# Causal mask of the two self attentions by extra contraction rows and small diagonal products, their maximum subtracted without GpSimd

## Chip, cores, metric

The kernel runs on one core of one Trainium2 chip. The metric is the device time of one execution in microseconds (us); lower is better. Most executions of one kernel agree within 0.3%, but the three timed runs of this one differ by more.

## What is computed

The reference is a decoder of two blocks over x of 8 sequences x 128 tokens x 256 features: block 0 is a causal self attention, a long convolution with gates and a mixture of experts; block 1 is a causal self attention, a masked cross attention and a routed mixture of experts. Each sublayer adds to x, behind a layer norm. The part that matters here, for both self attentions (16 heads of 16 features):

```python
scores = jnp.einsum('bqhd,bkhd->bhqk', Q, K)          # 1/sqrt(16) in all
scores = jnp.where(tril(ones(128, 128)), scores, -inf)
attn = softmax(scores, axis=-1)
out = jnp.einsum('bhqk,bkhd->bqhd', attn, V).reshape(B, S, D) @ Wo.T + bo
```

## The kernel before

Five engines run programs of their own, tied by semaphores (`S("name")`). The whole of x stays in SBUF. Order in time: self attention of block 0 (the list `FIRST`, call name SELF0), convolution, experts of block 0, then one pipeline (`SECOND`) that holds self attention of block 1 (SELF1, units from step 0) and cross attention (CROSS, units from step `CROSS_FROM` = 20), then the experts of block 1.

An attention is cut into units. A self attention has two units for each sequence, 16 in all, of eight heads each; the cross attention has 32 units. `attention(run)` of every engine walks the same steps t, and each engine does at step t what its lag says. On TensorE (all matmuls are issued by the helper `mm`, L1396, and f32 transposes by `tr`, L1400), step t does, in this order:

1. `less_max` of unit t-2 (L1521): eight products of 128 columns write minus the row maximum (and the mask) into the banks that take the scores by key. Stationary operand: `LMs`, which GpSimd made; moving: minus the identity, `negidb`.
2. `mask` of unit t (L1490): two products of 512 columns, identity times the mask repeated four times, start banks 0 and 1. Each waits until VectorE has read that bank (`att_mx`).
3. `scores` of unit t (L1511): eight products with 48 contraction rows (three terms of a split float16 product, 16 rows each), four at rows 0 to 47 into bank 0 and four at rows 64 to 111 into bank 1, alternating.
4. `scores_by_key` of unit t-2 (L1533): the same eight transposed, keys on partitions, on top of step 1's banks (2 to 4).
5. Transposes of x for the next sublayer, where due; `pv` of unit t-4 (exponentials times values, four column groups of 32); transposes of its result (lag 5); every second step the transposes and the product of the output projection (lags 6 and 7).

VectorE (`attention`, L1100) divides results, adds to x, takes the maximum over keys from banks 0 and 1 (two reductions, L1141) and does statistics and normalisation of x. ScalarE takes the exponential of banks 2 to 4 (L831) and copies from PSUM. GpSimd (L592) makes `LMs` = maximum minus mask for every unit of every attention (L614, two instructions), then `rstd` (L562, L563), low parts of float16 pairs (L585) and the bias rows (L581). SyncE issues the DMAs: `stack` (L447) waits for each quarter of the queries and keys and spreads it into the rows of `QS` and `KS`, 24 DMAs for each self attention, each into 16 partitions, twelve for each half of the tokens (`spread`, L445); half 0 gates unit 0 and half 1 gates unit 8. The constants (`ident`, `identb`, `negidb`, `causal`, `identh`, then `chgroup` and others) are made at the start on GpSimd (L574 to L645), each adding to `S("const")`.

## Time and profile before

| what | value |
|---|---|
| three timed runs | 585.8, 577.96, 586.9 us; median 585.8 us |
| profiled execution, device time | 583.44 us |
| its span, first to last instruction | 581.7 us (1.7 us lie around it) |
| mean granted TensorE clock | 0.974 |

The profile is one execution. Durations in it are its own; a number worked out from it is set against 583.44 us, not against the median.

### The profile page before, as it was taken

The page shows a single profiled execution, that of the slowest core. Times are in us where ns is not written, and L with a number is a line of the kernel's source. Part 1 is how long each engine was busy: PE and PEld are TensorE (multiplying, and loading weights), DVE is VectorE, ACT ScalarE, POOL GpSimd, SP SyncE. Part 2 cuts the span into 40 slices and gives each one's busy share as a digit, 9 for nine tenths or more (in the row PEclk, how much of TensorE's full clock was granted, in tenths as well). Part 3 has the DMA queues.
Part 4 walks back from the last instruction along what each step waited for, and adds up shares of the span by engine and source line. Part 5 has one row for each costly group of instructions (what it writes and reads, how often), then busy time and mean ns, then how long its engine had stood idle before and what let it go on. Part 6 is the DMA issues. An engine that isn't in the chain of part 4 may idle for free.

```text
span 581.7 us, 12908 instructions
## 1 busy us (share of the span) xinstructions
PE 537.3 (92%) x4838; PEld 338.2 (58%) x4838; DVE 363.7 (63%) x798; ACT 259.8 (45%) x533; POOL 316.2 (54%) x392
## 2 busy tenths in 40 slices
PE   7989998999699999999998889997999998989998
PEld 4546765444436666664665456664555554456687
DVE  5455864999846556452476478768577766963331
ACT  2315463000476666562445435655656567204430
POOL 3437854889664436321021579959899984450000
PEclk9988998999879999998999979999999999999999
DMA  7996019000006434331211995011130003017311
GB/s 251 133 145 257 3 55 406 2 0 0 1 2 187 120 98 108 93 109 68 75 50 25 124 150 220 3 29 29 29 101 1 3 7 158 1 53 306 139 40 64
DMA packets 25133, 53.04 MB, mean 91 GB/s; under 512 B 3515, under 2 KB 16333, under 8 KB 23153
## 3 DMA queue, kind: packets, MB, share of 16 engines
q1 hardware_dynamic: 24357, 51.01, 32.2%
q10 hardware_dynamic: 716, 1.21, 0.6%
q8 instruction: 40, 0.66, 0.5%
q14 instruction: 20, 0.16, 0.1%
HBM read 41.51 MB, written 1.12 MB: 73 GB/s over the span
## 4 chain that ended last, share of the span: by engine, by line
PE 61%; DVE 17%; POOL 8%; issue 4%; SPq 3%; DMA 3%; ACT 3%; POOLq 0%; DVEq 0%; ACTq 0%
PE PS L1396 55%; POOL R L614 6%; PE PS L1400 4%; DVE R L1242 4%; DVE R L1239 3%; SPq L445 2%; DVE mx L1141 2%; DVE R L424 2%; DMA R<-R 1%; DVE xn L1020 1%; DMA WT<-in_wt_a_dram 1%; PE PS L1419 1%; POOL rstd L563 1%; DVE X L1010 1%; DVE stats L1005 1%
## 5 line engine op out<-in xcount | busy, mean ns | idle before, releaser
L1396 PE MATMUL PS<-R 128*128 128x256 f16 (+5 forms) x1864 | 187.2, 277 | 2.2 <-DVE R L1298 1.4
L1396 PEld LDWEIGHTS PS<-R 128*128 128x128 f16 (+4 forms) x1864 | 125.3, 104 | 72.9 <-issue 46.9
L1141 DVE TENSOR_REDUCE mx<-PS 128x4 bf16<-128x512 f32 x128 | 82.3, 685 | 36.6 <-PE PS L1396 27.6
L831 ACT ACTIVATE R<-PS 128x512 f32<-128x512 f32 x128 | 69.4, 594 | 70.6 <-PE PS L1396 70.5
L1396 PE MATMUL PS<-xnT,R 128*128 128x512 f16 (+1 forms) x348 | 87.1, 392 | 2.1 <-ACT xnT L745 2.1
L614 POOL TENSOR_TENSOR R<-mx,causal 128x512 bf16<-128x512 bf16 x64 | 66.9, 1066 | 37.6 <-DVE mx L1141 36.8
L1289 DVE TENSOR_TENSOR R<-R,wr 128x512 f32<-128x512 f32 (+1 forms) x46 | 33.3, 724 | 58.9 <-ACT R L930 53.1
L614 POOL TENSOR_TENSOR R<-mx,R 128x512 bf16<-128x512 bf16 x64 | 65.4, 1045 | 6.4 <-DVE mx L1141 6.3
L930 ACT ACTIVATE R<-PS,small 128x512 f32<-128x512 f32 (+1 forms) x50 | 34.3, 685 | 50.8 <-PE PS L1396 50.8
L1396 PEld LDWEIGHTS PS<-xnT,R 128*128 128x128 f16 (+1 forms) x348 | 34.6, 101 | 36.7 <-issue 4.8
L1396 PE MATMUL PS<-negidb,R 128*128 128x128 bf16 x512 | 43.6, 225 | 3.9 <-POOL R L614 2.5
L562 POOL TENSOR_SCALAR veps<-mv 128x1 f32<-128x1 f32 (+1 forms) x30 | 7.2, 240 | 68.6 <-DVE mv L1006 68.6
L1396 PEld LDWEIGHTS PS<-negidb,R 128*128 128x128 bf16 x512 | 33.8, 100 | 14.3 <-POOL R L614 6.0
L1396 PE MATMUL PS<-R,VP 128*32 128x128 f32 (+2 forms) x608 | 38.8, 289 | 3.4 <-DVE R L424 2.5
L1298 DVE TENSOR_TENSOR R<-R 128x512 f16<-128x512 f32 (+1 forms) x50 | 37.1, 743 | 0.9 <-ACT R L918 0.7
L659 POOL TENSOR_TENSOR R<-xnT,ctxT 128x512 f32<-128x512 f32 x32 | 33.5, 1068 | 6.6 <-PE PS L1396 4.9
L1400 PE MATMUL PS<-ident,R 128*128 128x128 f32 (+1 forms) x168 | 32.1, 289 | 4.7 <-DVE R L1242 1.3
L1020 DVE TENSOR_SCALAR xn<-X,mv,rstd 128x256 f32<-128x256 f32 x48 | 28.5, 623 | 12.6 <-POOL rstd L563 12.3
L681 POOL TENSOR_TENSOR R<-R 128x256 f16<-128x256 f32 (+1 forms) x25 | 21.5, 859 | 26.0 <-ACT R L876 26.0
L678 POOL TENSOR_TENSOR R<-R 128x256 f16<-128x256 f32 (+1 forms) x25 | 19.0, 762 | 28.8 <-ACT R L871 28.8
L1010 DVE TENSOR_TENSOR X<-X,PS 128x256 f32<-128x256 f32 x48 | 19.8, 412 | 21.2 <-PE PS L1396 20.9
L918 ACT ACTIVATE R<-R 128x512 f16<-128x512 f32 (+1 forms) x50 | 31.0, 621 | 2.4 <-DVE R L1289 2.4
(206 smaller groups left out, 801.8 us busy)
## 6 DMA issues: line engine op xcount, KB each, us to landing
R<-in_experts_dram SPq DMA_DIRECT2D x5, 1536.0 KB, 8.9
R<-R SPq DMA_DIRECT2D x48, 128.0 KB, 6.3
wr<-g_scr SPq DMA_DIRECT2D x16, 256.0 KB, 3.2
R<-in_w_dram SPq DMA_DIRECT2D x1, 3200.0 KB, 18.3
R<-in_w_dram SPq DMA_DIRECT2D x1, 3168.0 KB, 11.1
WT<-in_wt_a_dram SPq DMA_DIRECT2D x2, 1024.0 KB, 11.8
R<-in_toe_dram SPq DMA_DIRECT2D x1, 2048.0 KB, 12.2
wr<-g_scr SPq DMA_DIRECT2D x10, 192.0 KB, 2.8
```

The lines of the kernel that those rows point to most:

```text
L614: g.tensor_tensor(LMs[:, n % 3, 4 * k:4 * k + 4, :], mx[:, n % 4, 4 * k:4 * k + 4].unsqueeze(2).broadcast_to([P, 4, P]), mask_of(c, u // c ...
L659: g.tensor_tensor(kv[:, h % 2, m, :].rearrange("p (b j i) -> p b j i", b=B, j=CI), v.unsqueeze(2).broadcast_to([P, B, CI, CI]), k.unsqueez ...
L831: s.activation(PTm[:, n % 4, 4 * k:4 * k + 4, :], bank(2 + (2 * n + k) % 3).rearrange("p (h q) -> p h q", h=4), ACT.Exp, scale=c["sc"]).th ...
L918: s.activation(hg16[0:m, i % 3, 0, :], h, ACT.Copy).then_inc(S("hg_hi"), 1)
L930: s.activation(hid[0:m, i % 4, :], bank(i % 2, parts=m), ACT.Relu, bias=b1col[0:m, blk:blk + 1]).then_inc(S("hid"), 1)
L1010: v.tensor_tensor(x, x, src, ALU.add).then_inc(S("x_updated"), 1)
L1020: v.tensor_scalar(xn[:, b, :], X[:, b, :], mv[:, b, 0:1], rstd[:, b:b + 1], ALU.subtract, ALU.mult).then_inc(S("ln_done"), 1)
L1141: v.tensor_reduce(mx[:, n % 4, 4 * k:4 * k + 4], bank(k).rearrange("p (h k) -> p h k", h=4), AX.X, ALU.max).then_inc(S("att_mx"), 1)
L1289: v.tensor_tensor(hg[0:m, i % 3, :], hid[0:m, i % 4, :], grow[0:m, n % 4, :], ALU.mult).then_inc(S("hg"), 1)
L1298: v.tensor_tensor(hg16[0:m, i % 3, 1, :], h, hg16[0:m, i % 3, 0, :], ALU.subtract).then_inc(S("hg16"), 1)
L1396: return nc.tensor.matmul(o_, l, r, start=start, stop=stop)
L1400: return nc.tensor.transpose(o_, i_, ident[0:k, 0:k])
```

## The change

In the self attentions alone (the cross attention keeps `mask`, `LMs` and GpSimd):

- The queries and keys get four more contraction rows (48 to 51 and 112 to 115, one for each block of 32 queries): 65504 at a query's own block, -65504 at keys of later blocks, so a key that lies in a later block of 32 gets -4.3e9 within the score products themselves, which have 52 rows then. `later_blocks` fills these rows by four DMAs from `blocks` (4 partitions, each piece of 128 float16 repeated 64 times) ahead of each `stack`.
- Within a block of 32, the mask is added by 32x32 products: `later_keys` (eight, 128 columns each) behind the scores, `later_keys_by_key` (eight) behind the scores by key. The four of a bank share a band of 32 contraction rows and lie in four column groups; the four banks use four different bands.
- The two 512-column products of `mask` go. The first score product of a bank starts it, and waits for `att_mx` in their place.
- `less_max` takes the maximum itself, `mx`, one column read 128 times (stride zero), as stationary operand, and waits for `att_mx` rather than for GpSimd.
- On TensorE `scores_by_key` of unit t-2 moves ahead of `scores` of unit t; the small products of t, then those of t-2, follow.
- GpSimd makes no `LMs` in the self attentions, and makes two more constants at the start.

```diff
+        causal_k = sb("causal_k", [P, P], BF16)
+        blocks = sb("blocks", [4, 2, P], F16)
...
-            return [(8 * (u % 2) + 2 * j + k, 64 * k, 48, 4 * (u % 2) + j) for k in range(2) for j in range(4)]
+            return [(8 * (u % 2) + 2 * j + k, 64 * k, 52, 4 * (u % 2) + j) for k in range(2) for j in range(4)]
...
+            def later_blocks(c):
+
+                for row in (48, 112):
+                    for which, to in ((0, QS), (1, c["KS"])):
+                        sp.dma_start(to[row:row + 4, :, :].rearrange("p g (b t) -> p (g b) t", b=B),
+                                     blocks[:, which:which + 1, :].broadcast_to([4, 8 * B, P])).then_inc(S("blocked"), 16)
+
+            sp.wait_ge(S("const"), 6)
+            later_blocks(SELF0)
             stack(SELF0)
...
+            sp.wait_ge(S("down0"), N0)
+            later_blocks(SELF1)
             stack(SELF1)
...
                     c, u = unit_at(run, t, 0)
-                    if c:
-                        if c is CROSS:
-                            pool.wait_ge(S("xmask"), 2)
-                        else:
-                            pool.wait_ge(S("const"), 4)
+                    if c is CROSS:
+                        pool.wait_ge(S("xmask"), 2)
...
             g.tensor_copy(identh[:, :], ident[:, :]).then_inc(S("const"), 1)
+
+            link(g.memset(causal_k[:, :], 0.0))
+            link(g.affine_select(out=causal_k[:, :], in_=causal_k[:, :], compare_op=ALU.is_ge, fill=NEG, base=0,
+                                 pattern=[[1, P]], channel_multiplier=-1))
+            link(g.memset(blocks[:, 0, :], HUGE))
+            link(g.affine_select(out=blocks[:, 0, :], in_=blocks[:, 0, :], compare_op=ALU.is_ge, fill=0.0, base=0,
+                                 pattern=[[1, P]], channel_multiplier=-QUARTER))
+            link(g.affine_select(out=blocks[:, 0, :], in_=blocks[:, 0, :], compare_op=ALU.is_ge, fill=0.0,
+                                 base=QUARTER - 1, pattern=[[-1, P]], channel_multiplier=QUARTER))
+            link(g.memset(blocks[:, 1, :], -HUGE))
+            g.affine_select(out=blocks[:, 1, :], in_=blocks[:, 1, :], compare_op=ALU.is_ge, fill=0.0, base=-QUARTER,
+                            pattern=[[1, P]], channel_multiplier=-QUARTER).then_inc(S("const"), 1)
...
-                        if n >= 4:
-                            dve.wait_ge(S("att_lm"), 2 * (n - 3))
+                        if c is CROSS and u >= 4:
+                            dve.wait_ge(S("att_lm"), 2 * (u - 3))
+                        elif n >= 4:
+                            dve.wait_ge(S("att_st"), n - 3)
...
+                    if c is not CROSS and u == 0:
+                        pe.wait_ge(S("blocked"), 64 * (1 + ATTENTIONS.index(c)))
...
+                def on_diagonal(i, row, corner):
+
+                    rows = slice(row, row + QUARTER)
+                    for first in range(0, P, QUARTER):
+                        cols = slice(first, first + QUARTER)
+                        ins = mm(PS[cols, i, :].rearrange("p (j w) -> p j w", j=4)[:, :, cols], identb[rows, rows],
+                                 corner[rows, rows].unsqueeze(1).broadcast_to([QUARTER, 4, QUARTER]), False, True)
+                    return ins
+
+                def later_keys(c, u):
+                    for k in range(2):
+                        ins = on_diagonal(k, QUARTER * k, causal)
+                    ins.then_inc(S("att_s"), 1)
+
+                def later_keys_by_key(c, u):
+                    n = number(c, u)
+                    for k in range(2):
+                        ins = on_diagonal(2 + (2 * n + k) % 3, QUARTER * (2 + k), causal_k)
+                    ins.then_inc(S("att_st"), 1)
...
                     for j in range(4):
                         for k in range(2):
+                            if c is not CROSS and j == 0 and n >= 1:
+                                pe.wait_ge(S("att_mx"), 2 * n + k - 1)
...
-                        pe.wait_ge(S("att_lm"), i + 1)
+                        if c is CROSS:
+                            pe.wait_ge(S("att_lm"), 2 * u + k + 1)
+                        else:
+                            pe.wait_ge(S("att_mx"), i + 1)
...
-                            mm(PS[:, 2 + i % 3, j * P:(j + 1) * P],
-                               LMs[:, n % 3, 4 * k + j, :], negidb[:, :], j == 0, False)
+                            most = (LMs[:, n % 3, 4 * k + j, :] if c is CROSS
+                                    else mx[:, n % 4, 4 * k + j:4 * k + j + 1].broadcast_to([P, P]))
+                            mm(PS[:, 2 + i % 3, j * P:(j + 1) * P], most, negidb[:, :], j == 0, False)
...
                     c, u = unit_at(run, t, 0)
+                    if older and older is not CROSS:
+                        scores_by_key(older, of)
                     if c:
-                        mask(c, u)
+                        operands_ready(c, u)
+                        if c is CROSS:
+                            mask(c, u)
                         scores(c, u)
-                    if older:
+                    if c and c is not CROSS:
+                        later_keys(c, u)
+                    if older is CROSS:
                         scores_by_key(older, of)
+                    elif older:
+                        later_keys_by_key(older, of)
```

## Rows read from the trace of the kernel before

**Rows 1.** The page: busy time by engine, and TensorE's granted clock in 40 slices.
```profile
PE 537.3 (92%) x4838; PEld 338.2 (58%) x4838; DVE 363.7 (63%) x798; ACT 259.8 (45%) x533; POOL 316.2 (54%) x392
...
PEclk9988998999879999998999979999999999999999
```
**Rows 2.** Timeline, step 9 to 10 of SELF0: start us, us, engine, line, operands, count.
```profile
61.62 0.61 PE L1396 MATMUL PS<-negidb,R 128*128 128x128 bf16 x8
...
62.07 0.59 PE L1396 MATMUL PS<-causal,identb 128*128 128x512 bf16 x2
...
62.60 0.62 PE L1396 MATMUL PS<-R 48*128 48x128 f16 x16
...
63.15 0.64 PE L1396 MATMUL PS<-R,VP 128*32 128x128 f32 x16
...
64.86 0.61 PE L1396 MATMUL PS<-negidb,R 128*128 128x128 bf16 x8
...
67.82 0.61 PE L1396 MATMUL PS<-negidb,R 128*128 128x128 bf16 x8
```
**Rows 3.** Timeline of TensorE in a window of 0.02 us at 63.15.
```profile
63.15 0.32 PE L1396 MATMUL PS<-R,VP 128*32 128x128 f32 x4
```
**Rows 4.** Busy time in two windows: from:to, length, PE, PEld, DVE, ACT, POOL, clock.
```profile
60.00:80.00 20.00, 20.00 (x323) 14.21 (x323) 16.59 (x39) 10.87 (x26) 15.24 (x20) 1.00 0.01 3
36.00:47.00 11.00, 8.91 (x82) 4.60 (x80) 5.15 (x8) 2.17 (x4) 7.36 (x8) 0.69 1.11 232
```
**Rows 5.** Timeline at the start of SELF0, with [idle before <-releaser].
```profile
35.88 0.60 PE L1396 MATMUL PS<-causal,identb 128*128 128x512 bf16 x2 [0.52 <-DVE VP L1063]
...
36.93 1.29 DVE L1141 TENSOR_REDUCE mx<-PS 128x4 bf16<-128x512 f32 x2 [1.10 <-PE PS L1396]
...
39.10 1.29 DVE L1141 TENSOR_REDUCE mx<-PS 128x4 bf16<-128x512 f32 x2 [0.89 <-PE PS L1396]
39.86 0.23 PEld L1396 LDWEIGHTS PS<-negidb,R 128*128 128x128 bf16 x4 [0.71 <-POOL R L614]
...
44.90 1.29 DVE L1141 TENSOR_REDUCE mx<-PS 128x4 bf16<-128x512 f32 x2 [1.90 <-PE PS L1396]
```
**Rows 6.** Timeline of VectorE at the start of SELF1.
```profile
334.42 1.29 DVE L1141 TENSOR_REDUCE mx<-PS 128x4 bf16<-128x512 f32 x2 [1.92 <-PE PS L1396]
...
338.25 1.78 DVE L1080 MEMSET wr<- 128x2064 f32 x1 [0.38 <-issue]
...
345.13 1.29 DVE L1141 TENSOR_REDUCE mx<-PS 128x4 bf16<-128x512 f32 x2 [0.29 <-issue]
```
**Rows 7.** Groups by form, TensorE's and GpSimd's, 350 to 380 us, and one wait.
```profile
L614 POOL TENSOR_TENSOR R<-mx,causal 128x512 bf16<-128x512 bf16 x20 | 21.7, 1106 | 2.8 <-DVE mx L1141 2.7
...
L1419 PE MATMUL PS<-identh,R 128*128 128x128 f16 x8 | 0.8, 217 | 1.0 <-POOL R L585 1.0
```
**Rows 8.** Timeline: SyncE's first stack, GpSimd's last constant ahead of it, SELF1's start.
```profile
13.68 0.29 POOL L636 CAST identh<-ident 128x128 f16<-128x128 f32 x1
...
15.91 7.83 SPq L445 DMA_DIRECT2D R<-R  x12
...
308.25 2.80 PE L1396 MATMUL PS<-R 128*128 128x256 f16 x24 [1.36 <-DVE R L1298]
...
316.69 9.05 SPq L445 DMA_DIRECT2D R<-R  x12
...
333.40 0.59 PE L1396 MATMUL PS<-causal,identb 128*128 128x512 bf16 x2 [1.36 <-DMA R<-R]
```
**Rows 9.** DMA totals, 317 to 333 us, then 381 to 391 us: packets, MB, share.
```profile
DMA packets 2162, 1.99 MB, mean 124 GB/s; under 512 B 235, under 2 KB 2161, under 8 KB 2161
q1 hardware_dynamic: 2161, 1.97, 98.7%
...
q1 hardware_dynamic: 864, 0.39, 15.8%
```

More of the change, by code:

```diff
@@ L33 @@
 FAR = -3.0e38
+HUGE = 65504.0
+QUARTER = 32
 HF = 512
@@ L230, in decoder_kernel @@
         rp1 = pb1[:, 0:B * 36].rearrange("p (b e) -> p b e", b=B)
-        warm = sb("warm", [P, 1])
+        warm = VP[:, 1008:1009]
         wtmp = vl1
@@ L335, in unit_heads @@
                         for k in range(2) for j in range(4)]
-            return [(8 * (u % 2) + 2 * j + k, 64 * k, 48, 4 * (u % 2) + j) for k in range(2) for j in range(4)]
-        def mask_of(c, b):
-            return xmask[:, b, :] if c is CROSS else causal[:, :]
+            return [(8 * (u % 2) + 2 * j + k, 64 * k, 52, 4 * (u % 2) + j) for k in range(2) for j in range(4)]
         def first_products(c, half):
@@ L603, in attention @@
                     c, u = unit_at(run, t, 0)
[L604 to L608 removed]
+                    if c is CROSS:
+                        pool.wait_ge(S("xmask"), 2)
                         n = number(c, u)
[L610 to L611 removed]
+                        pool.wait_ge(S("att_st"), n - 2)
                         for k in range(2):
@@ L615, in attention @@
                                             mx[:, n % 4, 4 * k:4 * k + 4].unsqueeze(2).broadcast_to([P, 4, P]),
-                                            mask_of(c, u // c["upb"]).unsqueeze(1).broadcast_to([P, 4, P]),
+                                            xmask[:, u // c["upb"], :].unsqueeze(1).broadcast_to([P, 4, P]),
                                             ALU.subtract).then_inc(S("att_lm"), 1)
@@ L840, in attention @@
                     if run is SECOND and t == LAST_UNIT + 10:
-                        s.activation(warm[:, :], ident[:, 0:1], ACT.Sigmoid)
+                        s.activation(warm, ident[:, 0:1], ACT.Sigmoid)
             def router(part):
@@ L1489, in attention, with operands_ready @@
             def attention(run):
-                def mask(c, u):
-                    upb = c["upb"]
-                    b, first = divmod(u, upb)
+                def operands_ready(c, u):
+                    b, first = divmod(u, c["upb"])
                     if c is CROSS and first == 0 and b % 2 == 0:
@@ L1503, in mask @@
                         pe.wait_ge(S("qx_lo"), 2)
-                    m_ = mask_of(c, b)
+                    if c is not CROSS and u == 0:
+                        pe.wait_ge(S("blocked"), 64 * (1 + ATTENTIONS.index(c)))
+                def mask(c, u):
                     n = number(c, u)
                     for k in range(2):
-                        if n >= 1:
-                            pe.wait_ge(S("att_mx"), 2 * n + k - 1)
-                        mm(bank(k), identb[:, :], m_.unsqueeze(1).broadcast_to([P, 4, P]), True, False)
+                        pe.wait_ge(S("att_mx"), 2 * n + k - 1)
+                        mm(bank(k), identb[:, :], xmask[:, u // c["upb"], :].unsqueeze(1).broadcast_to([P, 4, P]), True, False)
+                def on_diagonal(i, row, corner):
[14 more added lines that the diff above has]
+                    ins.then_inc(S("att_st"), 1)
                 def scores(c, u):
+                    n = number(c, u)
                     ts = slice(u // c["upb"] * P, (u // c["upb"] + 1) * P)
@@ L1515, in scores @@
                         for k in range(2):
+                            if c is not CROSS and j == 0 and n >= 1:
+                                pe.wait_ge(S("att_mx"), 2 * n + k - 1)
                             _, row, rows, idx = unit_heads(c, u)[4 * k + j]
                             ins = mm(PS[:, k, j * P:(j + 1) * P], QS[row:row + rows, idx, ts],
-                                     c["KS"][row:row + rows, key_at(c, idx), ts], False, j == 3)
-                    ins.then_inc(S("att_s"), 1)
+                                     c["KS"][row:row + rows, key_at(c, idx), ts], c is not CROSS and j == 0,
+                                     c is CROSS and j == 3)
+                    if c is CROSS:
+                        ins.then_inc(S("att_s"), 1)
                 def less_max(c, u):
@@ L1546, in scores_by_key @@
                             _, row, rows, idx = unit_heads(c, u)[4 * k + j]
-                            ins = mm(PS[:, 2 + (2 * n + k) % 3, j * P:(j + 1) * P], c["KS"][row:row + rows, idx, ts],
-                                     QS[row:row + rows, idx, ts], False, j == 3)
-                    ins.then_inc(S("att_st"), 1)
+                            mm(PS[:, 2 + (2 * n + k) % 3, j * P:(j + 1) * P], c["KS"][row:row + rows, idx, ts],
+                               QS[row:row + rows, idx, ts], False, False)
                 def pv(c, u):
@@ L1681, in _ @@
             pe.wait_ge(S("small"), 16)
-            pe.wait_ge(S("const"), 6)
+            pe.wait_ge(S("const"), 7)
             pe.wait_ge(S("toe_loaded"), 16)
@@ L1792, in ranks @@
                 pe.wait_ge(S("selb1"), part + 1)
-                pe.wait_ge(S("const"), 8)
+                pe.wait_ge(S("const"), 9)
                 b0, b1 = PARTS[part]
```

3 lines of the change are left out of this document (1 added, 2 removed).

## Prediction

> **What bounds the kernel now.** I read the page first, then the two self attentions step by step. The page [rows 1] shows TensorE busy for 92% of the span; its clock dips below full speed in two slices that hold the starts of the self attentions, among others. In the middle of SELF0 (60 to 80 us in [rows 4]) TensorE is busy for all of 20 us, VectorE for 16.6, GpSimd for 15.2 and ScalarE for 10.9: here the time is TensorE's alone. The timeline of a pair of steps [rows 2] gives its pace: `less_max` begins at 61.62, 64.86 and 67.82, so two steps take 6.20 us. GpSimd's two instructions for each unit, about 1.04 us each, lie beside that and are not the bound. They bound at two kinds of place: at the start of each self attention, where the pipeline is not yet full (TensorE waits 0.71 us for L614 [rows 5]), and in SELF1, where GpSimd also has the low parts, so that transposes wait 1.0 us in all for L585 [rows 7], which stands behind L614.
>
> **What goes on TensorE.** From the first mask product (62.07) to the first score product (62.60) it is 0.53 us [rows 2]. Two products of 512 columns at 2.4 GHz stream for 0.43; the other 0.10 is the change from 128 rows to bands of 64, and stays (`less_max` still precedes a band of 64). Sixteen score products take 0.55 to the next group, 0.46 streaming (eight pairs of 128 columns) and 0.09 for the next change of shape.
>
> **What comes on TensorE.** Sixteen 32x32 products of 128 columns, in the shape of four bands by four column groups, which no row of before shows. Cost: one more change of shape, 0.09 to 0.10, and the products. Lower end: all hidden behind the streaming before them, 0. Upper end: one behind the other, 16 x 0.056 = 0.90 (0.46 us for eight pairs is 0.056 a pair). The nearest row is `pv`, which also sits in groups of 32 columns: four of its products, 0.30 us long each, fill 0.32 us together [rows 3], so they start within 0.02 us, some 0.007 apart. Sixteen at 0.007 is 0.11, plus the last one's 0.053 of streaming: I take 0.16. A step then loses 0.43 and gains 0.25: 0.18 less. This holds where TensorE sets the pace, units 5 to 15 of each: 22 x 0.18 = 4.0 us less. (Range of this term: 22 x (0.43 - 0.10) = 7.3 less, to 22 x (0.43 - 0.09 - 0.90), or 12.3 more.)
>
> A rule speaks against this. The Trainium skill, "TensorE: Matmul & The Clock Gate", Part 3, says that a weight load overlaps running matmuls only when its row group differs; the four products of a bank share one. By that rule they go one by one, the sum would be the upper end, and it is a rival below. The `pv` rows disagree, as all their products share all 128 rows and still start within 0.02 us.
>
> **The stationary operand with stride zero.** Eight loads a step, now hidden under the 0.056 us pace of `less_max` (0.45 us from 61.62 to 62.07 for eight [rows 2]). Lower end 0, as only the addresses change. Upper end: the load shows at double pace, 8 x 0.056 = 0.45 a step. I take 0: the shape and type are the same.
>
> **The starts.** In SELF0 the reductions of units 0 and 3 begin at 36.93 and 44.90 [rows 5], three steps in 7.97 us. What a step needs at least is VectorE's two reductions, 1.35 us with the gap, then scores 0.2, change 0.09, small products 0.06, and 0.33 from the last product to the reduction: 2.03, against 2.17 now (39.10 - 36.93). The next two steps wait for L614, then for the exponential, at a mean clock of 0.69 (36 to 47 us in [rows 4]), that is, partly at 1.2 GHz. Without GpSimd, and with 0.85 less of masks at 1.2 GHz for 0.4 more of small products and change, I make them 2.15 and 2.8: 6.98, so 1.0 less, and by estimate 0.3 more for the step behind them. In SELF1 four steps take 10.71 (334.42 to 345.13 [rows 6]); there a fill of 1.78 us on VectorE sits between the reductions and holds whatever GpSimd does, so only 0.4 goes. Sum: 1.7 less.
>
> **GpSimd in SELF1.** The 1.0 us of [rows 7] goes. What is late next is the normalisation on VectorE, which has slack. VectorE itself works 16.6 of 20 us [rows 4], about 5.1 in a pair of steps of 6.2; the new pair of 5.84 still holds it.
>
> **The tails.** Two steps of each attention have only older units: they have no mask to lose, but a change of shape and eight small products, 0.15 each: 0.6 more.
>
> **SyncE and the DMAs.** At the start, seven small GpSimd instructions come between `identh` (ends 13.97 [rows 8]) and the block DMAs. At some 0.35 us each, as its neighbours', they end at about 16.4; four issues follow at 0.65, so the first spread leaves at 19.1 in place of 15.91. In SELF1 the new wait for `down0` ends with TensorE's last down product at 311.05 [rows 8], while the first spread leaves at 316.69: behind the waiting SyncE is only `stack`, which waits longer anyway, and four issues fit.
>
> Moving is another matter. No row shows a DMA of 64 KB into 4 partitions in pieces of 256 B. From 317 to 333 us [rows 9] the queue is 98.7% busy and moves 124 GB/s, a spread of 131 KB into 16 partitions in 1.06 us. Lower end for a block DMA: half of that, 0.5. Upper end: four queues only, 64 pieces each at the mean packet of that stretch (0.987 x 16 x 16 us / 2161 = 0.117 us), 7.5. The nearest is the rate by rows: a quarter of the partitions at a quarter of the rate, 2.1 us, 8.5 for four. The Trainium skill, "DMA: Bandwidth & Descriptors", says in "How many engines (k)" that a DMA uses the largest number up to 16 that divides its slowest dimension, here four, and in "Specifications" that pieces under 512 B miss line rate; no run here shows either, and both lean to the upper end.
>
> With 2.1: in SELF0 the blocks are through at 16.6 + 8.5 = 25.1, and the twelve spreads left on the same queues (96 packets at 0.06 us, between 0.117 and the 0.029 of the stretch from 381 us, 0.158 x 16 x 10 / 864) at 30.9; unit 0 starts at 35.88 on VectorE's account [rows 5], so it costs 0.3 at most. In SELF1 311.3 + 8.5 = 319.8 reaches 2.5 us into a queue that is full, and unit 0 waits for it already (1.36 us at 333.40 [rows 8]): I take 1.0 more of the 0 to 2.5. Sum 1.3 more.
>
> **Sum.** -4.0 -1.7 -1.0 +0.6 +1.3 = -4.8. From 583.4 of the profiled execution that is 578.6. Its time lies 2.4 below the median of the three, from which the same sum gives 581.0. I name 580. The wait ahead of the cross attention (a chain of DMAs that starts from a query product in step 15) moves forward as a whole, so the gain is not lost there.
>
> **The rivals.**
>
> A. *The block DMAs hold the starts (slower).* Place: the queues that carry them, ahead of the spreads. With d for one, SELF0 starts late by 16.6 + 4d + 5.8 - 35.9 = 4d - 13.5, SELF1 by 311.3 + 4d + 5.8 - 333.2 = 4d - 16.1. Together they eat the 6.1 us of the other terms from d = 4.5 us, 0.070 us a piece on four queues. At d = 5.5 they cost 14.4: 583.4 - 6.1 + 14.4 = 591.7. For: pieces a quarter of those measured, few partitions, a queue that is already full. Against: pieces of 512 B take 0.029. Chance 0.13.
>
> B. *Small products go one by one.* 22 steps with 0.74 more, 16.3, and some 3 in starts and tails: 578.6 + 19 = 598. For: the rule above. Against: [rows 3]. Chance 0.06.
>
> C. *The stride-zero load shows.* Half its upper end, 0.22 in 32 units, 7 us: 586. For: nothing in the rows, it is only unseen. Against: same shape and type. Chance 0.09.
>
> D. *More goes.* The small products hide entirely (7.3), the cold stretches at the two starts shrink with GpSimd's wait (11 us at 0.69 are 3.4 us of clock; 1.2 of it at each start), the DMAs cost nothing: 583.4 - 7.3 - 1.7 - 2.4 - 1.0 + 0.6 = 571.6. For: the stretch at half clock begins where TensorE idles. Against: the reductions pace the start in any case. Chance 0.12.
>
> E. *GpSimd's time was the gain, and it was not on the path*: if the mask's columns were also hidden, nothing changes, 583 to 586. TensorE's 20.00 of 20 speaks against it; it is part of the forecast's range.
>
> **How the numbers follow.** The forecast 0.60 with its own range 575 to 586, A 0.13, D 0.12, C 0.09, B 0.06. The range reaches down to D and up to A: 571 to 592; beyond lie B, the far part of A and of D. A measurement of this kernel tells about 2% (11.7 us) from no change. Faster by more needs under 574: most of D, 0.12. Slower by more needs over 597.5: B and the end of A, 0.08. The rest 0.80.
>
> **What would show it right or wrong.** Right: no causal mask product, sixteen 32*32 products a step that take about 0.16 us from first to last, pairs of steps of 5.84 us; less_max still at 0.45 for eight; the first reduction of SELF0 at about 37, of SELF1 1 us later against its stack than now; L614 with 64 instructions only, no wait on L585 in SELF1. Wrong: DMA as releaser of unit 0 in SELF0, or over 3 us at SELF1 (A); small products 0.056 apart (B); less_max longer than 0.45 (C); pairs under 5.7 (D).

## The result: 2.4% slower

| | before | after |
|---|---|---|
| median of the runs | 585.09 us (4 runs) | 596.62 us (4 runs, 594.87 to 599.00) |
| ratio after to before | | 1.0243, 95% interval 1.0183 to 1.0303 |
| profiled execution, span | 583.44, 581.7 us | 594.87, 593.1 us |
| TensorE's mean granted clock | 0.974 | 0.960 |

The forecast was 580.0 with a range of 571 to 592, and 0.08 for slower by over 2%. The result lies outside, on the side of rival A. The ratios in this document are formed from the executions that ran undisturbed and the medians from all of them, so the two can differ by some tenths of a per cent. The page of after first; its lines answer to [rows 1]:

```profile
PE 533.7 (90%) x5286; PEld 341.8 (58%) x5286; DVE 358.3 (60%) x798; ACT 259.5 (44%) x533; POOL 251.6 (42%) x335
...
PEclk9985999999969999998999968999999999999999
```

TensorE is busy for 3.6 us less and GpSimd for 64.6 less, so the parts that were to go did go; and TensorE's share falls from 92 to 90%, so it waits more. The two dips of the clock are deeper. Where the time went is read from the moments at which VectorE starts the first reduction of a unit (us of the profiled executions; the last column is a kernel told of below):

| stretch | before | after | blocks by engines |
|---|---|---|---|
| start to SELF0's first reduction | 36.93 | 45.34 | 38.43 |
| SELF0, unit 0 to unit 15 | 41.80 | 41.82 | 39.88 |
| to SELF1's first reduction | 255.69 | 260.65 | 254.04 |
| SELF1, unit 0 to unit 15 | 44.21 | 42.70 | 44.07 |
| to the cross attention's first | 13.68 | 13.36 | 13.39 |
| from there to the end | 189.4 | 189.2 | 190.8 |

Of the 11.4 us in the span, 8.4 arise ahead of SELF0's first unit and 5.0 ahead of SELF1's. TensorE's last down product begins at 308.25 in before [rows 8] and at 315.60 in after, 7.35 later, and the first reduction of SELF1 comes 13.4 later: 6.0 us arise at that start alone, 1.1 having been made up between. 1.8 come back in the self attentions and the link to the cross attention. The timeline at both starts of after, SyncE and then the units, against [rows 5, 6, 8]:

```profile
16.10 7.27 SPq L471 DMA_DIRECT2D R<-blocks  x4
23.49 20.59 SPq L446 DMA_DIRECT2D R<-R  x24
...
44.35 0.61 PE L1418 MATMUL PS<-R 52*128 52x128 f16 x8 [8.69 <-DMA R<-R]
...
45.34 1.29 DVE L1163 TENSOR_REDUCE mx<-PS 128x4 bf16<-128x512 f32 x2 [9.21 <-PE PS L1418]
47.66 1.29 DVE L1163 TENSOR_REDUCE mx<-PS 128x4 bf16<-128x512 f32 x2 [1.04 <-PE PS L1418]
...
52.68 1.29 DVE L1163 TENSOR_REDUCE mx<-PS 128x4 bf16<-128x512 f32 x2 [1.41 <-PE PS L1418]
...
318.42 7.52 SPq L471 DMA_DIRECT2D R<-blocks  x4
326.06 21.12 SPq L446 DMA_DIRECT2D R<-R  x24
...
346.83 0.61 PE L1418 MATMUL PS<-R 52*128 52x128 f16 x8 [7.46 <-DMA R<-R]
```

A DMA is now the releaser of unit 0 in both, after 8.69 and 7.46 us of idle TensorE; the prediction had named this as the sign of rival A. SyncE needs 7.27 us to issue four block DMAs (0.84, 0.66, 2.49 and 3.15 one by one), and the first spread leaves at 23.49. What the queues did meanwhile, DMA totals of after from 17.5 to 31 us:

```profile
DMA packets 1285, 0.52 MB, mean 39 GB/s; under 512 B 1068, under 2 KB 1281, under 8 KB 1281
...
q1 hardware_dynamic: 1283, 0.50, 24.8%
```

and from 18 to 23 us, when only pieces of the blocks move:

```profile
q1 hardware_dynamic: 403, 0.10, 19.1%
```

The four block DMAs are 1024 packets of 256 B. They run from 17.5 to 31.1 us: 3.4 us a DMA. While they are alone, the sixteen engines are busy for 19.1% of their time, three engines' worth, so most of them stand idle; if the pieces lie on four queues, each queue starts one every 0.053 us. Behind them the spreads stand, 128 packets of 1 KB each: the first such packet starts at 27.05 though its DMA was issued at 23.49, and at 31.0 only 213 packets are through, less than two spreads' worth. From about 33 us a spread's worth takes 1.03 us, close to the 1.06 of before [rows 9]; the twelfth is reached at 41.2 (in before at 29.3), and unit 0 starts at 44.35. That the four queues which carried the blocks end last would explain the 3 us between; no view shows the queues one by one. At SELF1 the blocks' pieces move from 319.8 to 334.2 us, 3.6 us a DMA, and unit 0 starts 12.6 us after their end, at SELF0 13.3 us after it: about twelve times the 1.06 us of a spread in both.

In the middle of SELF0, where TensorE sets the pace, against [rows 2]:

```profile
62.23 0.61 PE L1418 MATMUL PS<-negidb,mx 128*128 128x128 bf16 x8
62.77 0.62 PE L1418 MATMUL PS<-R 52*128 52x128 f16 x16
63.32 0.25 PE L1418 MATMUL PS<-causal,identb 32*32 32x128 bf16 x8
63.34 0.25 PE L1418 MATMUL PS<-causal_k,identb 32*32 32x128 bf16 x8
63.52 0.64 PE L1418 MATMUL PS<-R,VP 128*32 128x128 f32 x16
...
71.19 0.61 PE L1418 MATMUL PS<-negidb,mx 128*128 128x128 bf16 x8
74.20 0.61 PE L1418 MATMUL PS<-negidb,mx 128*128 128x128 bf16 x8
76.93 0.61 PE L1418 MATMUL PS<-negidb,mx 128*128 128x128 bf16 x8
```

Two steps take 5.74 us (71.19 to 76.93) in place of 6.20. The sixteen small products with the next change of shape take 0.20 us (63.32 to 63.52), and `less_max`, now with the stride-zero operand, 0.54 to the next group with its change of shape, thus still about 0.45 for eight. Rivals B and C are out by these rows. So the steps are shorter by 0.23, and yet units 0 to 15 of SELF0 take as long as before. The busy time in windows shows why: from:to, length, PE, PEld, DVE, ACT, POOL, clock, DMA share, GB/s; of after, then of before:

```profile
60.00:80.00 20.00, 18.66 (x423) 14.42 (x424) 13.97 (x36) 10.74 (x25) 1.59 (x4) 1.00 0.27 107
40.50:58.00 17.50, 11.77 (x192) 8.09 (x192) 6.44 (x10) 3.53 (x7) 0.00 (x0) 0.51 1.14 177
344.00:362.00 18.00, 12.99 (x224) 8.70 (x224) 9.20 (x14) 3.86 (x8) 0.00 (x0) 0.53 1.08 148
```

```profile
40.00:47.00 7.00, 6.51 (x58) 3.59 (x56) 2.97 (x5) 2.17 (x4) 5.26 (x6) 0.52 1.08 294
337.00:344.00 7.00, 6.14 (x55) 3.60 (x56) 5.07 (x7) 2.06 (x4) 4.88 (x6) 0.52 1.04 117
```

The clock drops to its lower level, 1.2 GHz, at 40.8 us, 5 us into the wait for the DMAs, and stays there until 57.8: 17.1 us in place of 6.8, and the same again at SELF1. The first eight steps of SELF0 take 21.9 us, against 20.3 in before, and the seven behind them 19.9 against 21.5: the start gives back what the masks save; a hole of 1.04 us at 66.41, told of at the end, is among them.

### The profile page after: what moved, and what is told of

It is laid out like the page before. It is cut to its first block and busy times, and to the rows that moved or that the text cites. A ratio compares the mean times of both kernels' runs of the same rounds, so it can differ in the third digit from the quotient of the medians.

```text
span 593.1 us, 13725 instructions
## 1 busy us (share of the span) xinstructions
PE 533.7 (90%) x5286; PEld 341.8 (58%) x5286; DVE 358.3 (60%) x798; ACT 259.5 (44%) x533; POOL 251.6 (42%) x335
## 5 line engine op out<-in xcount | busy, mean ns | idle before, releaser
L1418 PE MATMUL PS<-R 128*128 128x256 f16 (+5 forms) x1864 | 190.2, 281 | 22.4 <-DMA R<-R 16.1
L1418 PEld LDWEIGHTS PS<-R 128*128 128x128 f16 (+4 forms) x1864 | 126.7, 106 | 84.9 <-issue 51.2
L1418 PE MATMUL PS<-R,VP 128*32 128x128 f32 (+2 forms) x608 | 40.1, 297 | 3.9 <-DVE R L425 2.5
L1030 DVE TENSOR_TENSOR X<-X,PS 128x256 f32<-128x256 f32 x48 | 19.8, 412 | 21.5 <-PE PS L1418 21.2
L698 POOL TENSOR_TENSOR R<-R 128x256 f16<-128x256 f32 (+1 forms) x25 | 19.1, 763 | 29.0 <-ACT R L891 29.0
L1040 DVE TENSOR_SCALAR xn<-X,mv,rstd 128x256 f32<-128x256 f32 x48 | 24.9, 547 | 10.8 <-POOL rstd L575 10.2
L1418 PEld LDWEIGHTS PS<-R,VP 128*32 128x32 f32 (+1 forms) x608 | 21.8, 110 | 16.5 <-DVE R L425 3.9
L891 ACT ACTIVATE R<-R 128x256 f16<-128x256 f32 (+1 forms) x25 | 10.3, 410 | 47.2 <-PE PS L1418 45.6
L1422 PEld LDWEIGHTS PS<-ident,R 128*128 128x128 f32 (+1 forms) x168 | 17.2, 139 | 16.8 <-issue 8.9
```

The lines of the kernel that those rows point to most:

```text
L1040: v.tensor_scalar(xn[:, b, :], X[:, b, :], mv[:, b, 0:1], rstd[:, b:b + 1], ALU.subtract, ALU.mult).then_inc(S("ln_done"), 1)
L1418: return nc.tensor.matmul(o_, l, r, start=start, stop=stop)
L1422: return nc.tensor.transpose(o_, i_, ident[0:k, 0:k])
```

## The experiments

The theory was: the DMAs of the block rows make the loss, and the lower clock behind them takes back part of the gain. Rivals: the small products and the longer contraction cost; SyncE's held issue and not the queues; GpSimd's part was off the path. All ratios are to the kernel before on the same chip.

**Without the block rows, twice.** The rows and their DMAs are left out, the contraction is 48 rows again; everything else is as in after, so the mask is applied on the diagonal 32x32 blocks only.

```diff
-            return [(8 * (u % 2) + 2 * j + k, 64 * k, 52, 4 * (u % 2) + j) for k in range(2) for j in range(4)]
+            return [(8 * (u % 2) + 2 * j + k, 64 * k, 48, 4 * (u % 2) + j) for k in range(2) for j in range(4)]
-            sp.wait_ge(S("const"), 6)
-            later_blocks(SELF0)
-            sp.wait_ge(S("down0"), N0)
-            later_blocks(SELF1)
-                    if c is not CROSS and u == 0:
-                        pe.wait_ge(S("blocked"), 64 * (1 + ATTENTIONS.index(c)))
```

> The kernel after without the four block rows and their DMAs (48 contraction rows again): later blocks of 32 are left unmasked, all else stays. Theory 1 (the block DMAs are the loss): the first reductions fall back to about 37 us and 334 us or earlier, the loss of 14.4 us at the two starts goes, and the total is 577 to 580 us, 1% under the kernel before. Theory 2 (TensorE's clock is the loss: it ran at half clock for 17.1 us at each start against 6.8 before, since the mask products no longer fill it): the starts come back but the half-clock stretches stay near 17 us and units 0 to 15 of SELF0 still take 41.8 us; total 581 to 585 us.

Measured: 581.89 us, ratio 0.9989 (0.9933 to 1.0045). The time lies in the range of theory 2. Its profiled execution took 762.09 us at a mean clock of 0.646 and tells nothing of where the time goes, so the same kernel ran once more:

> The kernel after without its block rows and their eight DMAs, once more, for a usable profile (the block rows' work is left out, so the output lacks the causal mask off the diagonal 32x32 products). Theory 'DMAs and clock': the first reductions are back at 36 to 37 us and 332 to 334 us, the steady pair of steps stays at 5.7 to 5.8 us, but the half-clock stretch at each start stays longer than the 6.8 us of before (10 us or more), and this takes back what the steps gain: 580 to 583 us. Rival 'DMAs alone': the stretches are back at about 6.8 us and the time is 577 to 579 us.

Measured: 579.99 us, ratio 0.9909 (0.9861 to 0.9956). Against the 1.0243 of after, 2.5% and 3.3% are gone, 15 and 19 us, with the same small products and the same stationary operand. The two ratios of this one kernel, on two chips, also differ by 0.8% between themselves; so a difference of that size between kernels on different chips shows nothing. The steps stay short; first reductions of its profiled execution, VectorE:

```profile
40.83 1.29 DVE L1159 TENSOR_REDUCE mx<-PS 128x4 bf16<-128x512 f32 x2 [0.77 <-PE PS L1414]
...
339.41 1.29 DVE L1159 TENSOR_REDUCE mx<-PS 128x4 bf16<-128x512 f32 x2 [0.76 <-PE PS L1414]
```

40.83 is not the 36 to 37 that was expected: this profiled execution is the longest of its ten (588.70 us), and a half-clock stretch lies at 10.9 to 17.7 us, in the products ahead of the first unit. 339.41 isn't the 332 to 334 expected either: a further stretch of 13.7 us lies at 270.3, where before has one of 3.4. No DMA is the releaser of unit 0. The stretches at the starts are 6.8 and 10.2 us, one as the rival had it and one as the theory had it, and the time lies between the two ranges: this run doesn't decide between them. Over the ten executions of this kernel the span goes from 572.9 us at a mean clock of 0.982 to 587.0 at 0.953, over the 25 of before beside it from 577.6 at 0.985 to 589.0 at 0.968. Where both ran at 0.976, this kernel had spans of 574.4 and 574.8 and before 582.1; but its mean clock is 0.967 and that of before 0.976. So the kernel with less work for TensorE ran at a lower mean clock. That this eats part of the gain is argued only; the kernels with fillers below raise the clock, and the time doesn't follow.

**Before, with the constants and the DMAs alone.** Nothing reads the rows; TensorE waits for them as in after.

```diff
+            sp.wait_ge(S("const"), 6)
+            later_blocks(SELF0)
             stack(SELF0)
...
+            sp.wait_ge(S("down0"), N0)
+            later_blocks(SELF1)
             stack(SELF1)
```

> The kernel before with only the constants, the four block DMAs ahead of each stack and the waits for them added (the rows they fill are not read). Theory 1: first reductions near 45 us and 348 us as in the kernel after, total 598 to 602 us, slower than the kernel after itself (596.6). If the loss is in the new products or the clock, the starts move by under 3 us each and the total is under 591 us.

Measured: 598.88 us, ratio 1.0313 (1.0271 to 1.0355), within the 598 to 602 expected. The constants and the DMAs make more than the whole loss: 16.7 us over before. The first reductions come at 46.78 and 350.09. Timeline:

```profile
15.84 7.64 SPq L474 DMA_DIRECT2D R<-blocks  x4
23.61 21.03 SPq L449 DMA_DIRECT2D R<-R  x24
...
46.78 1.29 DVE L1168 TENSOR_REDUCE mx<-PS 128x4 bf16<-128x512 f32 x2 [10.22 <-PE PS L1423]
```

**The queues or the issue: pieces of 1 KB, and GpSimd's queue.** In the first kernel GpSimd lays the pattern four times side by side ahead of the DMAs; in the second GpSimd issues the DMAs, so that SyncE's spreads never stand behind them.

```diff
-                                     blocks[:, which:which + 1, :].broadcast_to([4, 8 * B, P])).then_inc(S("blocked"), 16)
+                                     wide[:, which:which + 1, :].broadcast_to([4, 16, 512])).then_inc(S("blocked"), 16)
```

> The kernel after with the block pattern repeated four times in SBUF first (GpSimd, one copy), so that the block DMAs carry pieces of 1 KB, 16 for each partition, instead of 64 of 256 B. Theory 1a (SyncE is held while it issues: 7.3 us for four now, so that the spreads start late on all 16 queues): each issue takes under 1 us, the first spread leaves at about 20.5 us, first reduction at 37 to 39 us; total 582 to 587 us. Theory 1b (four queues are busy with 64 KB each whatever the pieces, and the spreads wait behind them): first reduction at 41 us or later, total 589 us or more.

```diff
-                        sp.dma_start(to[row:row + 4, :, :].rearrange("p g (b t) -> p (g b) t", b=B),
+                        g.dma_start(to[row:row + 4, :, :].rearrange("p g (b t) -> p (g b) t", b=B),
```

> The kernel after with the block DMAs, pieces of 256 B as they are, issued by GpSimd on its own queue instead of SyncE. Theory 1a (SyncE held at issue): the first spread leaves at 16 us again and the first reduction comes at 36 to 39 us; total 580 to 586 us. Theory 1b (the carrying queues are the limit): the spreads share them with the blocks, first reduction at 42 us or later, total over 590 us.

Measured: 593.22 us, 1.0169 (1.0074 to 1.0265), for pieces of 1 KB; 598.42 us, 1.0303 (1.0214 to 1.0393), for GpSimd's queue. Timelines of the one and of the other:

```profile
17.09 5.83 SPq L472 DMA_DIRECT2D R<-wr  x4
23.04 19.78 SPq L447 DMA_DIRECT2D R<-R  x24
...
42.10 0.42 PE L1428 MATMUL PS<-R 52*128 52x128 f16 x8 [4.50 <-DMA R<-R]
```

```profile
16.30 3.51 POOL L651 DMA_DIRECT2D R<-blocks  x4 [0.32 <-POOL blocks L644]
17.61 7.74 SPq L446 DMA_DIRECT2D R<-R  x2
...
44.15 0.61 PE L1418 MATMUL PS<-R 52*128 52x128 f16 x8 [6.30 <-DMA R<-R]
```

With GpSimd's queue the first spread leaves at 17.61, six us earlier, and unit 0 starts at the same time as in after: when the first spread leaves is not the bound. Its pieces move from 19.57 on, but only 128 of them have started by 29.36. SyncE is held here too (0.69 us for the first spread, 7.00 for the second), so this run doesn't part the full queues from the issue that is held behind them. Pieces four times as long save 2.3 us of SELF0's start, not the 6 to 8 expected: unit 0 at 42.10 is what theory 1b had. From 19 to 23 us, with only such pieces moving, the engines are busy for 21.9% of their time, again under four of sixteen.

**GpSimd's part alone.** The kernel without block rows, with the maximum spread by GpSimd as in before.

```diff
-                            most = (LMs[:, n % 3, 4 * k + j, :] if c is CROSS
-                                    else mx[:, n % 4, 4 * k + j:4 * k + j + 1].broadcast_to([P, P]))
+                            most = LMs[:, n % 3, 4 * k + j, :]
```

> As the kernel without block rows, but with the maximum spread by GpSimd again (mask minus maximum as the stationary operand) in the self attentions, so the stride-zero operand is undone alone. Theory 'GpSimd's part was worth what was forecast' (1.4 us from the two starts and 1.0 us from the waits in the second self attention): 2 to 3 us slower than the kernel without block rows, steps within 0.03 us of its steps except in SELF1's start. Rival 'GpSimd was off the path': within 1 us of it. Second rival, 'the stride-zero operand costs TensorE something': faster than it by over 1 us.

Measured: 584.40 us, ratio 0.9969 (0.9921 to 1.0018), against 0.9909 for the kernel without block rows on the same chip: 3.5 us by the ratios, 4.4 by the medians. The intervals overlap, so its size is open, and whether it is more than the noise too; 2 to 3 were expected. The profiles show a place: units 0 to 15 of SELF1 take 45.56 us against 43.35, and those of SELF0 39.97 against 39.11. Groups by form, 350 to 380 us, of this kernel and then of the one without it, against [rows 7]:

```profile
L1437 PE MATMUL PS<-identh,R 128*128 128x128 f16 x8 | 0.8, 217 | 2.1 <-POOL R L593 2.1
```

```profile
L1437 PE MATMUL PS<-identh,R 128*128 128x128 f16 x8 | 0.8, 217 | 0.1
```

**More work for TensorE at the starts.** `keep_busy` adds products of 128x256 on a free bank, to see what the lower clock costs.

```diff
+                keep_busy(16)
                 products = turned_x = updates = transposed = asked = 0
...
+                    if t < 5:
+                        keep_busy(4)
```

> The kernel without block rows, plus products on a free bank that nobody reads: 16 of 128x256 just before the first unit of each attention run and 4 in each of its first five steps (36 in each run, about 0.1 us each at full clock). Theory 'clock': with TensorE busier there the half-clock stretches shrink to 4 us or less, units 0 to 15 of each self attention take 2 to 4 us less together, and the time is 3 to 6 us under that of the kernel without block rows: 575 to 579 us. Rival 'the first steps are bound by VectorE and ScalarE whatever the clock': the stretches shrink but the time stays within 1.5 us. Second rival, 'the fillers are in the way': units 0 to 4 get longer by 0.4 us each and the time is 2 us or more above.

Measured: 585.67 us, ratio 0.9987 (0.9938 to 1.0036), above the kernel without block rows by 4.6 us by the ratios, 5.7 by the medians; theory 'clock' is out. The second rival had the time, but not the place: the first four steps aren't longer. Start of SELF0:

```profile
39.50 1.92 PE L1414 MATMUL PS<-ident 128*128 128x256 bf16 x16 [0.52 <-DVE VP L1079]
...
42.07 1.29 DVE L1159 TENSOR_REDUCE mx<-PS 128x4 bf16<-128x512 f32 x2 [2.63 <-PE PS L1414]
```

The stretches at both starts are gone, the mean clock is 0.980, and units 0 to 15 of SELF0 take 38.49 us against 39.11, 0.6 less with the fillers' own price in it. The first four steps are 1.3 us shorter (8.22 against 9.49) and the next four 0.7 longer, with two short waits of TensorE marked "issue" among them. The sixteen ahead of unit 0 stood in no idle time, since without the block DMAs TensorE doesn't wait there; they cost 1.9 us a start. Without them:

> The kernel without block rows and with the same five times four products, without the 16 ahead of the first unit. If the 16 explain why the run with them was 4.9 us above the kernel without block rows (two starts of 1.9 us), this one is 3.5 to 5 us under that run: 578 to 580 us of this chip's before at 583 to 585 us. If the four in each step are in the way, it stays within 1.5 us of that run, above 582 us.

Measured: 581.18 us, ratio 0.9895 (0.9855 to 0.9936): by the ratios, which here are of different chips, 5.4 us under the one with sixteen (4.5 by the medians) and level with the kernel without any. The time itself lies 1.2 us above the 578 to 580 expected.

**The block DMAs earlier.** The pattern is made first on GpSimd, and SELF0's four DMAs stand behind the loads of x and the first weights.

```diff
+            sp.wait_ge(S("made"), 1)
+            later_blocks(SELF0)
             sp.wait_ge(S("w_a0"), 16)
             load(ctxT[:, :, :], A["ctxT"], "ctxT_loaded")
...
-            sp.wait_ge(S("const"), 6)
-            later_blocks(SELF0)
             stack(SELF0)
```

> The kernel after with the first self attention's block constants made first on GpSimd and its four block DMAs issued right behind the loads of x and of the first weights (about 5 us) in place of 16.1 us; the second self attention is unchanged. Theory 'the DMAs' place': they are done by about 20 us, the first spread leaves at 16 to 18 us, SELF0's first reduction comes at 37 to 40 us (45.3 in the kernel after), SELF1's stays at 347 less the same amount, and the time is 588 to 592 us (596.6 for the kernel after). Rival 'it is not the place but the rows and products themselves': first reduction 43 us or later, 594 us or more.

Measured: 595.75 us, ratio 1.0163 (1.0080 to 1.0245), and the first reduction of SELF0 at 47.87, later than in after. The time of the rival came out, but not for its reason; timeline:

```profile
5.02 8.82 SPq L445 DMA_DIRECT2D R<-blocks  x4
...
8.40 0.40 ACTq L880 DMA_DIRECT2D small<-in_small_dram  x1
...
19.91 2.42 ACT L793 ACTIVATE R<-PS,small 128x512 f16<-128x512 f32 x4 [7.54 <-DMA small<-in_small_dram]
...
23.49 20.34 SPq L455 DMA_DIRECT2D R<-R  x24
```

The biases and scales (`small`, 219 KB, issued by ScalarE at 8.40) now move beside the pieces of the blocks, from 9.65 to 19.41 us (9.46 to 11.42 in after): ScalarE waits 7.54 us for them, and in after the same instruction begins at 13.75. The blocks' own pieces move from 10.2 to 27.3 us, so they still end behind the first spread's issue at 23.49, whose first piece moves at 29.1. The collision has reached the loads and has not left the spreads.

**The rows without DMAs.** The same block rows, written by engines. The pattern is laid over 128 partitions and copied over all of QS and KS, and the spreads overwrite what is theirs.

```diff
+            for w in range(2):
+                s.activation(*filled(SELF0, w, 0), ACT.Copy).then_inc(S("filla00"), 1)
             act.wait_ge(S("x_loaded7"), 16)
...
+            pool.wait_ge(S("down0"), N0)
+            for w in (1, 0):
+                g.tensor_copy(*filled(SELF1, w, 0)).then_inc(S("filla10"), 1)
             rstd_of(3, 4, 4)
```

and in the same way `filla01` and `filla11` for the second halves, ahead of the two loops of `add_row` on GpSimd; SyncE waits for a half's two copies ahead of its spreads.

> The kernel after with the same block rows, but written by engines in place of the eight DMAs: the pattern is laid out over 128 partitions (eight small GpSimd instructions right after ident) and copied over all of QS and KS, half by half, before the spreads overwrite the other rows: by ScalarE for the first halves of the first self attention (two copies of 128x2048, about 2.1 us each from the 0.63 us of 128x512, while it waits for x), by GpSimd for the rest (two copies each time, 3 to 5 us each). Theory 'only the DMAs were expensive': first reductions at 36 to 38 us (half-clock stretch in the products ahead of it: 40 to 41) and 332 to 340 us as without block rows, steady pairs 5.74 us, time within 2 us of the kernel without block rows, 578 to 583 us, so level with or a little under the kernel before. Rival 'the copies are in the way too' (GpSimd's copies hold the reciprocal roots that VectorE waits for, or the spreads wait for them): a start later by 3 us or more, 584 us or more.

Measured: 581.86 us (before: 583.40), ratio 0.9920 (0.9880 to 0.9961). It is below both kernels; below before by 0.8%, as much as one kernel's ratio changed between two chips above, and this one ran on one chip only. Timeline:

```profile
4.22 3.71 ACT L886 ACTIVATE R<-blocks 128x2048 f32<-128x2048 f32 x2 [1.94 <-POOL blocks L594]
...
15.88 3.73 POOL L666 COPY R<-blocks 128x2048 f32<-128x2048 f32 x2
16.96 21.53 SPq L453 DMA_DIRECT2D R<-R  x24
38.43 1.29 DVE L1171 TENSOR_REDUCE mx<-PS 128x4 bf16<-128x512 f32 x2 [0.77 <-PE PS L1426]
...
309.48 3.73 POOL L725 COPY R<-blocks 128x2048 f32<-128x2048 f32 x2 [4.07 <-PE PS L1426]
...
315.06 19.67 SPq L453 DMA_DIRECT2D R<-R  x24
...
332.35 1.29 DVE L1171 TENSOR_REDUCE mx<-PS 128x4 bf16<-128x512 f32 x2 [1.48 <-PE PS L1426]
```

Two copies for a half of QS and KS, 16 times what the rows alone would need (128 partitions for 8), take 3.7 us on ScalarE or GpSimd, beside other work. They stand in place of the four DMAs' 13.5 us. The first reduction comes 1.5 us later than in before, behind a half-clock stretch of 3.4 us at 11.2 us; in the next kernel, with the same copies and no such stretch, it comes at 36.32, 0.6 earlier than in before. A pair of steps takes 5.75 us here with 52 contraction rows (66.81 to 72.56) and 5.74 with 48 in the kernel without block rows (68.45 to 74.19): the longer contraction costs nothing.

> As the one before, with four 128x256 products on a free bank in each of the first five steps of each attention run, and nothing ahead of the first unit. In the run with 16 more ahead of it, those 16 took 1.9 us of each start and the half-clock stretches at the starts were gone, with units 0 to 15 no more than 1 us shorter. Theory 'the starts' clock is worth 1 to 2 us each': 2 to 3 us under the one before. Rival 'not measurable': within 1 us of it.

The same with the four products in each of five steps: 580.63 us, ratio 0.9954 (0.9915 to 0.9992). The mean clock over its eleven runs is 0.982, against 0.966 without the products, and the time is the same within what the runs tell: the rival's 'not measurable'.

**After, with TensorE kept busy in the wait.** As above, 48 ahead of the first unit and four in each of five steps, in the kernel after itself.

> The kernel after, with 48 products of 128x256 on a free bank ahead of the first unit of each attention run (about 5.2 us, within the 8.7 and 7.5 us in which TensorE waits for the DMAs there) and four in each of the first five steps. It splits the loss at the starts into the wait and the clock that falls in it. Theory 'wait and clock': the two half-clock stretches of 17.1 us at the starts shrink to 7 us or less, units 0 to 8 take 18.6 to 20 us in place of 21.9 us in SELF0, the first reductions stay at 45 and 346 us, and the time is 591 to 595 us (the kernel after was 596.6 against a before of 585.1; this chip's may shift both). Rival 'the clock costs nothing there': stretches shrink and the time stays within 1 us of 596.6. Second rival: the stretches do not shrink.

Measured: 599.19 us, ratio 1.0267 (1.0207 to 1.0327), not the 591 to 595 of the theory; the clock rose from 0.957, the mean of after's four runs, to 0.973, and the time didn't fall. TensorE at SELF0's start:

```profile
35.96 5.41 PE L1418 MATMUL PS<-ident 128*128 128x256 bf16 x48 [0.52 <-DVE VP L1083]
43.95 0.40 PE L1418 MATMUL PS<-R 52*128 52x128 f16 x8 [2.57 <-DMA R<-R]
...
58.21 0.64 PE L1418 MATMUL PS<-R,VP 128*32 128x128 f32 x4 [3.49 <-issue]
```

The wait for the DMA ends at 43.95, as in after (44.35), whatever TensorE does meanwhile; the half-clock stretches are 3.4 and 6.8 us in place of 17.1, and three of the first four steps are short (2.05 to 2.06 in place of 2.33; the other takes 2.89). But in the fifth, TensorE stands still for 3.49 us with "issue" as the reason. So what the lower clock costs at the starts isn't cleanly measured. An estimate for four steps is to be had from rows above: units 0 to 4 of SELF0 take 10.02 us in after, at the lower level throughout, and 8.22 in the kernel without block rows with 16 and 4 fillers, at full clock: 1.8 us. In the time of a whole kernel nothing of it shows; the products that lift the clock have a price of their own.

## Why the prediction was wrong, by its own steps

- **The step that failed is the DMA term**, 1.3 us forecast for both starts against 8.4 + 6.0 measured. It has three parts. (a) The size: 2.1 us for a block DMA by the rate by rows, 3.4 and 3.6 measured. (b) "The first spread leaves at 19.1": it left at 23.49; the kernel with GpSimd's queue shows that this isn't the bound. (c) "96 packets at 0.06 us", 5.8 us for the twelve spreads behind the blocks. It priced the twelve as what their packets add on the four queues, as if the other queues had gone on with the spreads meanwhile. Nearly all of the twelve ran after the blocks, at the full price, and the row for it stood in the prediction itself: 1.06 us a spread, 12.7 for twelve. Neither (a) nor (c) makes the loss by itself, as SELF0's start had some 5 us to spare in the forecast's sum: with 3.4 alone, rival A's formula gives 0.1 us (4 x 3.4 - 13.5); with 12.7 alone, 16.6 + 8.5 + 12.7 - 35.9 = 1.9; with both, 7.0, and from the blocks' real start 17.5 + 13.5 + 12.7 = 43.7, where unit 0 started at 44.35. So rival A had the place and the releaser right, and its formula, with the same 5.8, would have called a DMA of 3.4 us harmless. By the Trainium skill, "DMA: Bandwidth & Descriptors", "How many engines (k)", such a DMA gets four engines. The 19.1% of sixteen while the blocks are alone fits in four and is far from sixteen; the forecast had noted the rule and not let it move the value.
- **SELF1's start.** "Reaches 2.5 us into a queue that is full" made 1.0 us of it, and 6.0 were measured. It is the same two errors: with 3.6 for a DMA and 12.7 for the spreads, 311.3 + 14.4 + 12.7 - 333.2 = 5.2.
- **Masks.** -0.18 a step forecast, -0.23 measured. The mechanism of the small products and of the stride-zero operand was as forecast; a change of shape and sixteen products take 0.20 us, not 0.25. By the Trainium skill, "TensorE: Matmul & The Clock Gate", Part 3, a weight load overlaps only where row groups differ, and the small products of one row group would have gone one by one; sixteen in 0.20 us with the change of shape disagree. The span model of the same Part, some 4 ns for each further tile, would have the last of sixteen start 0.06 us after the first; 0.05 was measured.
- **Starts.** Three steps of SELF0 from 7.97 to 6.98: 6.99 in the kernel with blocks by engines. Four steps of SELF1, 0.4 less: 0.37 there (10.71 to 10.34). In after itself 7.34, at the lower clock throughout: the forecast had let that stretch shrink or stay, and it grew from 6.8 to 17.1 us behind the new wait.
- **GpSimd in SELF1.** 1.0 us forecast; with GpSimd's part put back the wait is 2.1, without it 0.1. In time the part is not clear of the noise.
- **The sum.** Without the DMA term it was -6.1 us. The kernel with the rows written by engines is at -0.8% of 583.4, that is -4.7 us (interval 2.3 to 7.0 less). What is missing to 6.1 can be placed in part: SELF1's eighth step takes 4.93 us in that kernel and 2.59 in before, with 2.16 us of the kind of hole told of below. That this is all of it isn't shown.

## What to carry to other kernels

A constant that is written by DMA is not free because it is small: price its pieces by a measured DMA of that shape (here 3.4 us for 64 KB), and put the whole of that ahead of everything that is issued behind it, at the full serial price of those transfers; then take off the time by which they could have been late without harm. Look for an engine that idles at that point before adding a DMA to a queue that something waits for; a copy over all partitions that later transfers overwrite can be much cheaper than the few rows alone. Fillers where TensorE isn't idle cost their own time, and here those in its idle time gained nothing either; don't take a higher mean clock for a gain.

## What the runs showed of the hardware

- Four partitions in pieces of 256 B: 64 KB in 3.4 us, or 19 GB/s; 0.053 us a piece if on four queues. Four of them take SyncE 7.3 us to issue, and each of the first two spreads behind them 3 us more (2.91 and 3.11).
- Sixteen 32x32 products in a grid of four by four start within 0.05 us of each other (from 66.90 us on in after).
- A broadcast operand of stride zero loads as fast as a dense one: eight `less_max` take 0.54 us to the next group with a change of shape of about 0.09, and 0.45 in before, where none follows.
- TensorE's holes with "issue" as the reason: in after this one, in the step of unit 8,

```profile
65.13 0.23 PE L1418 MATMUL PS<-R 52*128 52x128 f16 x2
66.41 0.57 PE L1418 MATMUL PS<-R 52*128 52x128 f16 x14 [1.04 <-issue]
```

  and the 3.49 us above. In each case a 16 KB packet of the instruction queue had landed 1.4 us before TensorE went on (at 65.02 and 56.78; 1.2 us for the hole of 2.16). Seven further holes of over 1 us, in the kernels without block rows and in those with fillers, end 1.3 to 1.5 us behind such a packet; before has none over 0.8 us in its self attentions. After has 448 more products and as many more loads than before, and the fillers add to them, while the loads of the next stage fill the queues (71.9% busy from 62 to 66 us). That the instructions came too late is argued from these times; no run took it away.
